# The second expert stage starts on its first batch while the head softmax still ends

## What is computed

```
x = x + attention(ln(x)); x = x + ffn(ln(x)); x = x + ssm(ln(x)); x = x + ffn(ln(x))
x = x + linear_attention(ln(x)); x = x + experts(ln(x))
x = x + head_softmax_attention(ln(x)); x = x + experts(ln(x))
```

```
dp = einsum('bhqd,bhkd->bhqk', q, k) * SCALE
attn = softmax(dp, axis=1)            # over the heads
out = (attn @ v, heads joined) @ w_proj + b_proj
```

## Time and profile before

| | before |
|---|---|
| runs | 2286.49, 2296.20, 2295.32 us, median 2295.32 |
| the profiled execution, its own time | 2285.96 us |
| its span | 2284.2 us |
| TensorE busy | 1869.8 us, 82% |
| VectorE busy | 1675.7 us, 73% |
| ScalarE busy | 1107.3 us, 48% |
| GpSimd busy | 1022.5 us, 45% |
| mean granted TensorE clock | 0.919 of full speed |

### The profile page before, as it was taken

The page is one execution under the profiler, slowest core; times in us unless marked ns, Lnnn a source line. Parts: engine busy times, 40 slices in busy tenths (PEclk is TensorE's granted clock), DMA queues, the critical chain, the costliest instruction groups (busy, mean ns, idle before and its releaser), DMA issues.

```text
span 2284.2 us, 32109 instructions
## 1 busy us (share of the span) xinstructions
PE 1869.8 (82%) x12288; PEld 1210.5 (53%) x12288; DVE 1675.7 (73%) x2158; ACT 1107.3 (48%) x1830; POOL 1022.5 (45%) x382
## 2 busy tenths in 40 slices
PE   7988999854888885559999977788878777499998
PEld 5444444343444444447777754455555455377776
DVE  4655556255899985547777689999999999467666
ACT  2344445421634322115555566666676766355554
POOL 3476767411277750110000048788888999300000
PEclk8898999876999997669999999899999999699999
DMA  2112111000200000011010000000000000100000
GB/s 70 29 38 48 29 29 29 1 10 11 37 0 0 1 1 10 5 47 42 15 37 19 1 1 1 1 1 1 2 1 2 1 2 1 42 28 28 14 1 19
DMA packets 34014, 37.53 MB, mean 16 GB/s; under 512 B 5763, under 2 KB 21382, under 8 KB 33862
## 3 DMA queue, kind: packets, MB, share of 16 engines
q1 hardware_dynamic: 33334, 34.43, 6.0%
q10 hardware_dynamic: 528, 1.05, 0.2%
HBM read 19.48 MB, written 1.05 MB: 9 GB/s over the span
## 4 chain that ended last, share of the span: by engine, by line
PE 40%; issue 19%; DVE 19%; POOL 14%; ACT 4%; DMA 2%; SPq 1%; POOLq 0%; DVEq 0%; ACTq 0%; PEldq 0%
PE ps L46 9%; PE ps L47 8%; PE ps L48 7%; DVE negm L2122 7%; POOL AF L685 6%; POOL hc L1274 3%; POOL AF L1274 3%; PE ps L489 2%; PE ps L473 2%; PE ps L514 1%; DVE AF L2129 1%; PE ps L853 1%; POOL AR_plain L1982 1%; DVE AR L1063 1%; DVE AR L1057 1%
## 5 line engine op out<-in xcount | busy, mean ns | idle before, releaser
L1083 DVE TENSOR_TENSOR AF<-ps,AF 128x512 f32<-128x512 f32 x256 | 176.9, 691 | 182.8 <-ACT AF L1037 181.9
L2122 DVE TENSOR_REDUCE negm<-ps 128x64 bf16<-128x1024 f32 x256 | 302.4, 1220 | 11.3 <-PE ps L1999 11.2
L685 POOL TENSOR_TENSOR AF<-AF 128x2048 f32<-128x2048 f32 (+3 forms) x73 | 234.2, 3209 | 153.8 <-ACT AF L625 147.8
L46 PE MATMUL ps<-XH,AR 128*128 128x512 f32 x616 | 257.1, 417 | 35.1 <-DVE AF L894 18.1
L1037 ACT ACTIVATE AF<-ps 128x512 f32<-128x512 f32 x256 | 152.9, 597 | 260.6 <-PE ps L48 258.6
L1982 POOL TENSOR_TENSOR AR_plain<-AF 128x2048 f32<-128x2048 f32 x64 | 261.8, 4092 | 38.2 <-ACT AF L2076 37.4
L2096 ACT ACTIVATE AF<-ps 128x1024 f32<-128x1024 f32 x192 | 196.5, 1023 | 146.6 <-PE ps L2008 144.8
L47 PE MATMUL ps<-XL,AR 128*128 128x512 f32 x616 | 248.0, 403 | 0.0
L48 PE MATMUL ps<-XH,AR 128*128 128x512 f32 x616 | 247.3, 402 | 0.0
L2008 PE MATMUL ps<-negm,ident_bf 128*128 128x512 bf16 x512 | 161.0, 397 | 96.3 <-DVE negm L2122 96.1
L625 ACT ACTIVATE AF<-ps 128x512 f32<-128x512 f32 (+1 forms) x304 | 155.6, 576 | 146.0 <-PE ps L476 82.8
(11 more groups left out here) (309 smaller groups left out, 3948.2 us busy)
## 6 DMA issues: line engine op xcount, KB each, us to landing
AR<-AR SPq DMA_DIRECT2D x96, 128.0 KB, 2.4
AF<-in_L_ffn_Wg_dram SPq DMA_DIRECT2D x19, 256.0 KB, 2.7
AF<-in_L_ffn_Wu_dram SPq DMA_DIRECT2D x19, 256.0 KB, 3.0
AF<-in_L_ffn_Wd_dram SPq DMA_DIRECT2D x19, 256.0 KB, 3.8
AF<-AF SPq DMA_DIRECT2D x16, 64.0 KB, 2.4
AF<-AR_plain SPq DMA_DIRECT2D x16, 64.0 KB, 2.4
out_dram<-X SPq DMA_DIRECT2D x1, 1024.0 KB, 5.1
AF<-in_L_attn_a_Wq_dram SPq DMA_DIRECT2D x1, 512.0 KB, 4.0
```

Source lines behind the costliest of these rows:

```text
L46: pe.matmul(out, ah, bh, start=start, stop=False)
L685: pool.tensor_tensor(zacc[u % 2][:, :, c0:512], zacc[u % 2][:, :, c0:512], pt[t % 4][:, :, 0:w], ALU.add).then_inc(s0_zp, 1)
L1083: dve.tensor_tensor(mh[:, m % 3, :], bank(2 + m % 2), msg[:, m % 3, :], ALU.mult).then_inc(m_h, 1)
L2122: dve.tensor_reduce(negm6[:, j % 4, :], bank(2 * (j % 3), 2).rearrange("p (j q i) -> p q j i", j=HJ, i=2), mybir.AxisListType.XY, ALU.max, ...
```

## The change

- **Norm.** Batch 0's norm for stage 7 becomes a guest of the softmax: statistics on VectorE at halves 144 to 152, the power on GpSimd before tile 76, the scaling on ScalarE as `x * rstd + shift` at halves 160 to 163, transposes after tiles 84 and 86. GpSimd gets two small operations for `shift`. The scaling of batch 1 for stage 6 moves from VectorE to ScalarE too.
- **Weights.** The first two experts of stage 7 get buffers of their own (`early_raw`, `early_h`, `early_l`) and are loaded during the softmax; the first split is at halves 200 (ScalarE) and 203 (VectorE).
- **Start.** The first `up` waits for the last exponential (`s6_e`), not for the end of stage 6. Every `up` of both expert stages also waits for its quarter of the low parts (`ln_lo`).
- **Guests of stage 7.** The last three tiles' value products come after units 0, 2 and 5, the last projection after unit 10, the last addition at unit 12; then batch 1's statistics at 13 to 16, its norm at 19 and 20, its transposes at 20 and 21. The inverse of the last tile is a `reciprocal` on VectorE, and it waits for the product of tile 125.
- **Order of experts.** Stage 7 uses nearly the order of stage 5, with batch 1 later and ten loads and splits, not eight. Two of the four returns to `X` come after units 104 and 107.
- **Store.** The output goes in three DMAs, batch 0 first.

The diff, cut to its core (functions that only moved out of `s6_pe` and `s6_act` are left out):

```diff
+        def ln_half_shift(pool, link, h):
+            link(pool.tensor_tensor(shift[:, half(h)], mv[:, half(h), 0], rstd[:, half(h)], ALU.mult))
+            pool.tensor_scalar(shift[:, half(h)], shift[:, half(h)], -1.0, None, ALU.mult).then_inc(ln_shift, 1)
+
+        def ln_tiles_norm_act(act, k, tiles):
+            h = tiles[0] // HB
+            act.wait_ge(ln_shift, k + 1)
+            for t in tiles:
+                act.activation(R[:, t, :], X[:, t, :], ACT.Identity, scale=rstd[:, t:t + 1],
+                               bias=shift[:, t:t + 1]).then_inc(ln_norm, 1)
...
+        early_raw = [AF[:, 12288:12288 + WCOL], AF[:, 15744:15744 + WCOL]]
+        early_h = [AR[:, 10240:10240 + WCOL], AR[:, 10240 + 2 * WCOL:10240 + 3 * WCOL]]
+        early_l = [AR[:, 10240 + WCOL:10240 + 2 * WCOL], AR[:, 10240 + 3 * WCOL:10240 + 4 * WCOL]]
+        MSG = [[msg[:, j, :] for j in range(3)],
+               [AR_plain[:, o:o + 512] for o in (9728, 16384, 16896)]]
+        MH = [[mh[:, j, :] for j in range(3)], [AR_plain[:, 8192 + 512 * j:8704 + 512 * j] for j in range(3)]]
+        MHH = [[mhh[:, j, :] for j in range(3)], [AF_R[:, 8192 + 512 * j:8704 + 512 * j] for j in range(3)]]
+        MHL = [[mhl[:, j, :] for j in range(3)], [AF_R[:, 9728 + 512 * j:10240 + 512 * j] for j in range(3)]]
...
         SEQ = [[(0, 0, 0), (0, 1, 1), (0, 2, 2), (0, 3, 3), (1, 2, 2), (1, 3, 3), (0, 4, 4), (1, 4, 4),
                 (0, 5, 5), (0, 6, 6), (0, 7, 7), (1, 6, 6), (1, 7, 7), (1, 5, 8), (1, 0, 9), (1, 1, 10)],
-               [(b, e, e) for e in range(NE) for b in range(B)]]
+               [(0, 0, 0), (0, 1, 1), (0, 2, 2), (0, 3, 3), (1, 2, 2), (1, 3, 3), (0, 4, 4), (1, 4, 4),
+                (0, 5, 5), (1, 5, 5), (0, 6, 6), (1, 6, 6), (0, 7, 7), (1, 7, 7), (1, 0, 8), (1, 1, 9)]]
...
+        def down_bank(k, q):
+            return bank(5) if (k, q) == (1, 1) else bank(6 + q % 2)
...
         def moe_load(q, s):
             k = (s - 5) // 2
-            q.wait_ge(x_done, X_AFTER[s])
+            if s == 5:
+                q.wait_ge(x_done, X_AFTER[s])
             for l in range(N_LOADS[k]):
                 n = LOAD0[k] + l
                 e = EXPERT_OF[k][l]
+                if s == 7 and l == 0:
+                    q.wait_ge(s6_sc, 12)
+                if s == 7 and l == 1:
+                    q.wait_ge(s6_st, len(JOBS))
+                    q.wait_ge(s6_pv, NTI // 2)
+                if s == 7 and l == 2:
+                    q.wait_ge(s6_pp, NTI - 2)
                 wait(q, m_wl, n - 1)
-                w = mraw[:, n % 2, :]
+                w = raw_of(n)
...
         def moe_pe(pe, s):
             k = (s - 5) // 2
-            ln_pe(pe, s)
+            if s == 5:
+                ln_pe(pe, s)
 
             def up(n):
                 i, c, l = unit(k, n)
                 m = PER * k + n
                 if n % PAIR == 0:
                     pe.wait_ge(m_wl, l + 1)
+                pe.wait_ge(ln_lo, 4 * s + i + 1)
                 wait(pe, m_h, m - 1)
...
                 if c == 0:
                     wait(pe, m_acc, m // FE - 1)
-                mm3(pe, bank(6 + m // FE % 2), (wh[:, o:o + P], wl[:, o:o + P]),
-                    (mhh[:, m % 3, :], mhl[:, m % 3, :]), start=c == 0, stop=c == FE - 1).then_inc(m_d, 1)
-
-            pe.wait_ge(ln_lo, 4 * s + 4)
+                    if s == 7 and n < 4 * FE:
+                        pe.wait_ge(x_done, X_AFTER[7] - (1 if n < 3 * FE else 0))
+                mm3(pe, down_bank(k, n // FE), (wh[:, o:o + P], wl[:, o:o + P]),
+                    (MHH[k][m % 3], MHL[k][m % 3]), start=c == 0, stop=c == FE - 1).then_inc(m_d, 1)
+
+            if s == 5:
+                pe.wait_ge(ln_lo, 4 * s + 4)
+            else:
+                pe.wait_ge(s6_e, 2 * NTI)
             up(0)
             up(1)
             for n in range(PER):
...
+                else:
+                    s7_join_pe(pe, n)
             if s == 7:
-                for i in range(NT):
-                    moe_out_pe(pe, k, i, bank(i % 2))
-                    if i == 1:
-                        pe.wait_ge(x_done, X_AFTER[s] + 2)
+                for i in (2, 3):
+                    moe_out_pe(pe, k, i, bank(2 + i))
...
+        def moe_split_act(act, k, l):
+            n = LOAD0[k] + l
+            act.wait_ge((m_w, m_w2)[n % 2], 48 * (n // 2 + 1))
+            if l > 1:
+                act.wait_ge(m_d, PER * k + PAIR * (LAST_PAIR[k][l - 2] + 1))
+            if k and l == 0:
+                act.wait_ge(s6_st, len(JOBS))
+            if k and l == 1:
+                act.wait_ge(s6_s, NTI)
+            if k and l == 2:
+                act.wait_ge(s6_pv, NTI)
+            act.activation(high_of(n), raw_of(n), ACT.Copy).then_inc(m_wh, 1)
+
+        def moe_split_dve(dve, k, l):
+            n = LOAD0[k] + l
+            dve.wait_ge(m_wh, n + 1)
+            dve.tensor_tensor(low_of(n), raw_of(n), f32(high_of(n)), ALU.subtract).then_inc(m_wl, 1)
...
-        LN_AT = {at: job[1] for job, at in PLACED if job[0] == "x"}
+        LN_AT = {at: (6, job[1]) for job, at in PLACED if job[0] == "x"}
+        LN_AT.update({84: (7, 0), 86: (7, 1)})
...
+                    pool.wait_ge(ln_rstd, 2 * s + 2)
+                    ln_half_shift(pool, link, 1)
+                if m == 76:
+                    ln_half_rstd(pool, link, 7, 0)
+                    pool.wait_ge(ln_rstd, 2 * 7 + 1)
+                    ln_half_shift(pool, link, 0)
+                if m < NTI - 1:
+                    pool.wait_ge(s6_wi, m + 1)
+                else:
+                    pool.wait_ge(s6_wi_end, 1)
...
+        LATE_PV = {0: NTI - 3, 2: NTI - 2, 5: NTI - 1}
+        JOIN_TR = {20: 2, 21: 3}
+        JOIN_OUT = {104: 0, 107: 1}
+
+        def s7_join_pe(pe, n):
+            if n in LATE_PV:
+                for part in range(2):
+                    pv(pe, LATE_PV[n], part)
+            if n == 10:
+                project(pe, NB - 1)
+            if n in JOIN_TR:
+                ln_quarter_pe(pe, 7, JOIN_TR[n], bank(2 + JOIN_TR[n]))
+            if n in JOIN_OUT:
+                moe_out_pe(pe, 1, JOIN_OUT[n], bank(4 + JOIN_OUT[n]))
+
+        def s7_join_act(act, link, n):
+            if n == 8:
+                flush(act, link, NB - 1, (0, 1))
+            if n == 9:
+                flush(act, link, NB - 1, (2, 3))
+            if n - 2 in JOIN_TR:
+                ln_quarter_act(act, 7, JOIN_TR[n - 2], bank(2 + JOIN_TR[n - 2]))
+
+        def s7_join_dve(dve, link, n):
+            if n == 12:
+                head_out_dve(dve, NB - 1)
+            if n == 13:
+                dve.wait_ge(x_done, X_AFTER[7])
+                ln_tiles_stats(dve, link, range(HB, HB + 4))
+            if n == 15:
+                ln_tiles_stats(dve, link, range(HB + 4, NB))
+            if n == 16:
+                ln_half_aggr(dve, link, 1)
+            if n == 19:
+                ln_tiles_norm(dve, 7, range(HB, HB + 4))
+            if n == 20:
+                ln_tiles_norm(dve, 7, range(HB + 4, NB))
+            if n - 3 in JOIN_TR:
+                ln_quarter_dve(dve, 7, JOIN_TR[n - 3], bank(2 + JOIN_TR[n - 3]))
+            if n - 2 in JOIN_OUT:
+                moe_out_dve(dve, 1, JOIN_OUT[n - 2], bank(4 + JOIN_OUT[n - 2]))
+
+        def s7_ready_pool(pool, link, s):
+            ln_half_rstd(pool, link, s, 1)
...
-            for m in range(NTI - LAG, NTI):
-                pv(m, 0)
-                pv(m, 1)
+                    pv(pe, j // 2 - LAG, j % 2)
+            for part in range(2):
+                pv(pe, NTI - LAG, part)
...
+                if 26 <= j < 30:
+                    ln_tiles_norm_act(act, 0, range(HB + 2 * (j - 26), HB + 2 * (j - 26) + 2))
+                if 160 <= j < 164:
+                    ln_tiles_norm_act(act, 1, range(2 * (j - 160), 2 * (j - 160) + 2))
+                if j == 200:
+                    moe_split_act(act, 1, 0)
...
             invert(NTI - 2)
-            invert(NTI - 1)
-            flush(NB - 1, range(HS))
...
-                if j in (26, 28):
-                    ln_tiles_norm(dve, s, range(HB + 2 * (j - 26), HB + 2 * (j - 26) + 4))
+                if 144 <= j < 152 and j % 2 == 0:
+                    dve.wait_ge(x_done, X_AFTER[s] + HB)
+                    ln_tiles_stats(dve, link, range(j - 144, j - 142))
+                if j == 152:
+                    ln_half_aggr(dve, link, 0)
+                if j == 203:
+                    moe_split_dve(dve, 1, 0)
...
             denominators(NTI - 1)
-            add(NB - 1)
-            dve.wait_ge(x_done, X_AFTER[s + 1])
+            dve.wait_ge(s6_zs, NTI)
+            dve.wait_ge(s6_pp, NTI - 2)
+            dve.reciprocal(w6i[:, (NTI - 1) % 2, :], z6[:, (NTI - 1) % 2, :]).then_inc(s6_wi_end, 1)
...
-            sp.wait_ge(x_done, X_AFTER[upto])
-            sp.dma_start(out_dram, X[:, :, :]).then_inc(out_sem, 16)
-            sp.wait_ge(out_sem, 16)
+            sp.wait_ge(x_done, X_AFTER[7] + 2)
```

(52 more changed lines are left out.)

125 lines of the change are left out of this document (45 added, 80 removed).

## The result

The changed kernel took 2260.03 us (median of four runs, 2258.67 to 2261.89) and the kernel before, on the same chip, 2291.10 us (four runs, 2286.49 to 2296.20). The ratio is 0.9865, with a 95% interval of 0.984 to 0.9889: faster by 1.35%. The forecast was 2262 us. In the two profiled executions the gain is 26.9 us: a span of 2284.2 us became one of 2257.3.

A forecast was written before the change was run, and what follows sets the result against it. VectorE paces the softmax, TensorE the expert stage, with about 40 us of latencies between; -36.2 + 8.1 + 1.5 - 3.5 = -30.1 us gives 2255.9 (profiled) or 2265.2 (median); forecast 2262, range 2250 to 2277.

The forecast's parts named there:

- The start: Softmax to expert stage: first up follows the last exponential, low parts wait for GpSimd products, finish(1) ends earlier: -36.2 us.
- Guests in stage 7: Expert stage: value products, projection, batch 1's norm, returns and two more splits compete with a full TensorE: +8.1 us.
- The end: Kernel's end: fewer returns there (about -1.9) and a last store of only 256 KB (-1.6): -3.5 us.
- Guests in the softmax: Softmax: VectorE loses eight norm tiles, gains statistics, low parts and a weight split: +1.5 us, bounds -1 and +6.
- eight norm tiles leave: Softmax: VectorE loses eight norm tiles that cost 5.5 us through waiting for GpSimd; part of that not won.
- statistics and aggregation: Softmax: VectorE gains eight statistics, 1.64 us, and their aggregation, taken as 0.6 us.
- two low parts: Softmax: VectorE gains two low parts of 512 columns, 0.68 us each, together 1.3 us.
- the first weight split: Softmax: VectorE's split of the first weights, about 1.75 us plus 1 us of waiting: 2.75 us.
- Nothing blocks at the start: Stage 7's start: low parts run beside GpSimd and first value product hides; total gain 34 to 38 us; chance 0.18.
- Guests cost their full length: Stage 7 and softmax: guests find no gaps, so the gain is 19 us, 2276 against the median; chance 0.23.
- It doesn't start early: Stage 7's start: some wait holds up(0) or down_e(0) until 1956.56 us or later; total -12 to -20 us; chance 0.05.
- TensorE's clock: Stage 7: without the resting gap TensorE's clock falls; 286 us at 0.81 would cost 67 us, time 2332; chance 0.03.

The follow-up runs named there:

- e1_small: Changed kernel without seven eighths of GpSimd's last two products (tiles 126 and 127): 2257.06 us, ratio 0.9849 to the kernel before.
- e2_place: Changed kernel with batch 0's transposes for stage 7 after tiles 82 and 84, not 84 and 86: 2256.10 us in one execution.
- e3_norm_dve: Changed kernel with batch 1's eight norm tiles for stage 6 put back on VectorE: 2268.64 us in one execution.
- e5_waits: Changed kernel with the added low-part wait only before every fourth up of stage 7, none in stage 5: 2265.60 us in one execution.
- r2_place: Changed kernel with stage 7's low parts at tiles 82 and 84, not 84 and 86, run side by side: 2259.00 us, ratio 0.9851.
- e4_16loads: Changed kernel with stage 7 doing all experts of batch 0, then batch 1, sixteen loads and splits, not ten: 2269.67 us in one execution.
- r1_change: The changed kernel itself, unedited, run again: 2260.22 us, ratio 0.9861 to the kernel before.

## Why the prediction was right

**The start, -36.2, measured -36.45.** The first up came 0.05 us after the last exponential (forecast 0.2), the reciprocal had waited for its product, both low parts ended just behind a GpSimd product. The reciprocal took 0.95 us instead of 0.4, an error that didn't show, since the low part behind it had to wait for GpSimd anyway. The working gave 12.7 us; it was 12.38. The reading of stage 2's L1542, that such an instruction waits out the product, carried this, and e1_small shows it by taking the product away.

**Guests in stage 7, +8.1, measured +8.07 and, repeated, +6.1.** The nearness of the first is luck: four other executions that start the stage in the same way and end it as the change does (e2_place, e3_norm_dve, e5_waits, r2_place) stay within 0.3 us of the second. The 0.9 us for a split is what e4_16loads measured. Units 8 to 24 took 2018.56 - 1979.05 = 39.5 us, 4.7 more than twice 17.4, inside the 4 to 6 forecast. Where the sum was too high can be told roughly. Against the kernel before r1_change has lost 0.8 us by unit 8, 4.6 by unit 24 and 6.1 by the last; for the two value products, which stand ahead of unit 8, I had counted 2.3. The items weren't measured one by one.

**The end, -3.5, measured -4.5.** The 256 KB store landed in 2.4 us, where I took 3.5 from a load's 2.7 and allowed for more: 1.1 us, the whole difference.

**Guests in the softmax, +1.5, measured +4.8 and +5.9: the term that was mis-sized.** It stayed inside its bound of +6. The sign that I gave for it was missed: the last exponential should have come 0 to 4 us later than at 1945.25, and it came 5.97 later, and 10.06 in r1_change, which is past the 6 us at which I called the forecast wrong; of these 1.1 and 4.2 had gathered before the softmax began, which is why the stretch is the fairer measure. By the places at which the stage falls behind the kernel before, from the starts of VectorE's sums:

| part | forecast | first profile | r1_change |
|---|---|---|---|
| eight norm tiles leave (tiles 12 to 70) | -5.5, and part not won | -3.4 | -2.6 |
| statistics and aggregation (71 to 79) | +2.2 | +2.6 | +2.8 |
| two low parts (90 to 93) | +1.3 | +3.2 | +3.2 |
| the first weight split (100) | +2.75 | +2.5 | +2.5 |

Two things made the error. The norm tiles had cost 5.5 us of VectorE's time but not of the stage's (e3_norm_dve). And I priced the two low parts by their length on VectorE and didn't ask which instruction of TensorE waits for the second: the order had it, a wait for low parts at the head of a chunk of eight tiles, and e2_place shows that it is 2.0 of the 3.2 us. The split's 2.75 us were nearly right, waiting included: it took 2.53. To follow it:

```profile
1830.00 2.53 DVE L1084 TENSOR_TENSOR AR<-AF,AR 128x1536 fp32r<-128x1536 f32 x1
```

**The sum** was 26.9 us in the profiled pair against 30.1, and 31 in the medians against 33 (2295 to 2262); 2 to 3 us of the gain are missing. That 2262 came within 2 us of the median is luck: two of the first three runs lay 9 us or more over the profiled one, I chose a value between the two groups, and the changed kernel's four runs fell there. From the profiled run alone the sum gave 2255.9, from the median 2265.2; both miss by 4 to 5 us.

**The rivals.** *Nothing blocks at the start* fell: 2.29 and 3.98 us. e1_small is that case, and its trace shows what it would have been worth: 3.8 us at the start, and 2.5 by the last unit. *Guests cost their full length* fell in stage 7 (8.07 at most, against 10.5 for VectorE's guests alone) but nearly held in the softmax, where VectorE is full: there length is cost, and a wait comes on top. *It doesn't start early* fell in the first row of TensorE. *TensorE's clock* fell as a loss: 1.00 over 2000 to 2100 us. It is there in small, as 0.54 over six microseconds of the first profile.
